# Masks of the first attention pass moved from TensorE to VectorE, second scores laid out by half of the rows, and loads and steps retimed

## What is computed

```
x = x + 0.5 * ffn(layernorm(x))
x = x + attn(layernorm(x))
x = x + 0.5 * ffn(layernorm(x))

ffn:  probs = softmax(x @ router_w.T)                 # 8 experts
      w = probs, kept up to a cumulated share of 0.9
      out = sum over e of (silu(x @ gate_w[e].T) * (x @ up_w[e].T)) @ down_w[e].T * w[:, e]   # 512 wide
attn: q, k, v with biases; 16 query heads, 4 key heads, 16 wide
      q, k: rms norm over the head, rotary embedding, q times a gain per head
      softmax of causal scores q k / 4, times v; output matrix and bias
```

## Time and profile before

| | |
|---|---|
| median of three runs | 1202.97 us (1202.05 to 1203.33) |
| the profiled execution | 1202.81 us, its span 1200.7 us |
| TensorE matmuls busy | 1161.9 us, 97% |
| VectorE, ScalarE, GpSimd busy | 817.4, 577.9, 667.5 us |
| mean granted TensorE clock | 0.996 |

### The profile page before, as it was taken

The page is one execution under the profiler, slowest core; times in us unless marked ns, Lnnn a source line. Parts: engine busy times, 40 slices in busy tenths (PEclk is TensorE's granted clock), DMA queues, the critical chain, the costliest instruction groups (busy, mean ns, idle before and its releaser), DMA issues.

```text
span 1200.7 us, 22926 instructions
## 1 busy us (share of the span) xinstructions
PE 1161.9 (97%) x8321; PEld 701.3 (58%) x8321; DVE 817.4 (68%) x1577; ACT 577.9 (48%) x954; POOL 667.5 (56%) x737
## 2 busy tenths in 40 slices
PE   4899999998999999999999999999999999999998
PEld 2455555665556566566566665566665656656655
DVE  6888896668777777577677577677667555554444
ACT  3544544444554554654554555555555454333332
POOL 3545443367477577576676666666655545332232
PEclk9899999999999999999999999999999999999999
DMA  4311210000000000000000000000000000000000
GB/s 176 127 53 53 68 52 1 1 1 2 1 1 2 1 2 1 1 1 2 1 1 1 1 1 2 5 15 1 1 2 1 19 1 2 1 14 5 1 1 19
DMA packets 10108, 19.26 MB, mean 16 GB/s; under 512 B 2192, under 2 KB 6800, under 8 KB 10000
## 3 DMA queue, kind: packets, MB, share of 16 engines
q1 hardware_dynamic: 9136, 15.17, 3.8%
q10 hardware_dynamic: 864, 2.63, 0.6%
HBM read 15.70 MB, written 2.10 MB: 15 GB/s over the span
## 4 chain that ended last, share of the span: by engine, by line
PE 71%; DVE 5%; POOL 4%; issue 2%; ACT 1%; DVEq 0%; ACTq 0%; POOLq 0%
PE YB L302 21%; PE G L283 20%; PE U L283 20%; POOL RR L1125 2%; PE S L438 2%; PE S L464 1%; PE S L479 1%; PE S L370 1%; PE S L414 1%; PE S L416 1%; DVE TS L705 1%; PE S L410 1%; DVE TS L710 1%; POOL HS L1069 1%; DVE MXN L944 1%
## 5 line engine op out<-in xcount | busy, mean ns | idle before, releaser
L1069 POOL TENSOR_TENSOR HS<-TS,HS 128x512 f16<-128x512 f32 x256 | 300.1, 1172 | 411.1 <-ACT HS L538 409.8
L302 PE MATMUL YB<-W,HS 128*128 128x256 f16 x3036 | 374.6, 273 | 13.8 <-DVE X L726 12.8
L283 PE MATMUL G<-XS,W 128*128 128x512 f16 x1536 | 376.7, 381 | 0.6 <-ACT XS L568 0.4
L283 PE MATMUL U<-XS,W 128*128 128x512 f16 x1536 | 375.2, 380 | 0.0
L302 PEld LDWEIGHTS YB<-W,HS 128*128 128x128 f16 x3036 | 293.0, 98 | 90.3 <-DVE X L726 18.3
L705 DVE SCALAR_TENSOR_TENSOR TS<-TS,G 128x512 f32<-128x512 f32 x256 | 175.2, 684 | 227.7 <-ACT TS L531 227.5
L538 ACT ACTIVATE HS<-TS 128x512 f16<-128x512 f32 x256 | 161.1, 629 | 265.0 <-DVE TS L710 262.9
L531 ACT ACTIVATE TS<-G,TSC 128x512 f32<-128x512 f32 x256 | 175.5, 686 | 209.1 <-PE G L283 199.3
L283 PEld LDWEIGHTS U<-XS,W 128*128 128x128 f16 x1536 | 150.7, 98 | 183.1 <-issue 2.8
L283 PEld LDWEIGHTS G<-XS,W 128*128 128x128 f16 x1536 | 147.2, 98 | 133.3 <-issue 3.4
L710 DVE SCALAR_TENSOR_TENSOR TS<-TS,U 128x512 f32<-128x512 f32 x256 | 175.9, 687 | 28.8 <-DVE TS L705 1.4
(11 more groups left out here) (181 smaller groups left out, 877.8 us busy)
## 6 DMA issues: line engine op xcount, KB each, us to landing
room<-in_up SPq DMA_DIRECT2D x4, 512.0 KB, 3.2
out_y<-X SPq DMA_DIRECT2D x16, 128.0 KB, 1.7
X<-in_x SPq DMA_DIRECT2D x3, 512.0 KB, 5.6
room<-in_gate SPq DMA_DIRECT2D x3, 512.0 KB, 3.2
room<-in_down SPq DMA_DIRECT2D x3, 512.0 KB, 3.6
QKT<-in_gate SPq DMA_DIRECT2D x3, 512.0 KB, 3.6
QKT<-in_up SPq DMA_DIRECT2D x3, 512.0 KB, 3.3
QKT<-in_down SPq DMA_DIRECT2D x3, 512.0 KB, 4.1
```

The source lines that it names most:

```text
L283: mm = eng.matmul(bank[:, :], W[:, e, wl, jj, kk * I + m * P:kk * I + (m + 1) * P], flat(XS16[:, b % 2, xl, kk, :, :], 'cq'), start=q == 0 ...
L302: mm = eng.matmul(out, HS[:, j % 2, hl, kk, m * P:(m + 1) * P], W[:, e, wl, 2, kk * D:(kk + 1) * D], start=kk + hl + wl == 0, stop=kk == K ...
L1069: eng.tensor_tensor(HS[:, j % 2, 1, m, :], TS[:, k % 3, :], HS[:, j % 2, 0, m, :], ALU.subtract).then_inc(L['g_lo'].sem, 1)
```

## The change

- **First scores.** `pe_max` has no mask matmuls and signals S0 and S1 separately. `dve_max` has one `tensor_tensor_reduce` for each head: scores plus mask, written back to the bank in place, with the negated extremum as a second output. `MB` gets a second, unmasked half for the 256 keys of an odd tile. `dve_mm` runs a slot later (`MM_STEP`).
- **Second scores.** S1 takes rows 64 to 127 and S0 rows 0 to 63 of key tile 0, both query tiles at once (512 columns, one matmul each). S2 still holds key tile 1 against query tile 1, with a matmul of each half of 256 columns, the second behind a wait. `pool_mask('a')` covers the query-tile-0 half of both blocks in one instruction, so `act_ph('b')` waits for it. `pe_pv` reads P in the new layout.
- **Steps.** The offsets of the conversions, of the rms norm (`sq`, `rb0`, `ss` a slot earlier), of `ax`, `ql`, `bo` and of the router change as the tables show; `dve_r2` is cut in two. `PREP` starts expert 2 at slot 8 and ends at 72 and 83.
- **Start.** SP issues all early loads: x 0 and 1, x 2 and 3, `gate`; after x 2 and 3 have landed, `up`, x 4 to 7, `down`, the router's weights, experts 1 and 2, then x's rest. ScalarE issues none. `pe_wb0(0)` stands ahead of the first transposes, and the third matrix's scale is found in slots 1 to 5, in YB.
- **Waits.** `s0_read`, `s1_read` and `s2_read` name only entries that used the bank. `RWR` and `LOW` are stored elsewhere or narrower.

```
-PREP = [-99, 0, 12, 24, 36, 47, 58, 69, 82]
+PREP = [-99, 0, 8, 24, 36, 47, 58, 72, 83]
...
+AT = {'at': (108, 114, 16, 33), 'qkv': (110, 116, 21, 39), 'qt': (117, 124, 30, 48), 'kt': (118, 125, 32, 48), 'q2': (125, 137, 48, 69)}
+MAX0 = (119, 122, 126, 128, 130, 132)
+MAXB = (38, 41, 50, 56, 59, 66)
+OUT = (5, 15)
+FTP0 = (3, 3, 6, 6)
+FIRST_FTP = (99, 102, 104, 109, 152, 152, 161, 161)
+FTP_LATER, ROUTE_LATER = (22, 24)
+ROUTE_FIRST = (3, 11, 112, 162)
+
+A_STEP = {'ax': 3, 'xl': 3, 'bo': 6}
+Q_STEP = {'rb1': 2, 'sq': 2, 'rb0': 2, 'rr': 3, 'r': 4, 'qn': 5, 'qz': 4, 'v': 5, 'qh': 6, 'ql': 6}
+I_STEP = {'eb': 1, 'ea': 1, 'ma': 2, 'ec': 2, 'hb': 3, 'mc': 3, 'ha': 4, 'lb': 4, 'hc': 5, 'la': 4, 'lc': 5, 'pv': 7, 'o': 8}
+R_STEP = {'r1': 1, 'ex': 1, 'r2': 1, 'r2b': 3, 'rank': 3, 'r3': 5}
+F_STEP = {'xn': 1, 'xh': 2, 'xl': 3}
+O_STEP = {'ot': 2, 'mm': 2, 'ad': 3}
+MM_STEP = 2
+
+W_FIRST = {'mx': 1, 'wt': 2, 'wr': 4, 'wb': 5, 'sc': 5, 'hi': 6, 'lo': 6}
...
-QKVP = by_tile(110, 116, 21, BATCH + 3)
-QTP = by_tile(118, 124, 30, BATCH + 12)
-KTP = by_tile(118, 124, 32, BATCH + 12)
-QTP2 = by_tile(125, 136, BATCH + 12, BATCH + 33)
...
-    MAXS += [[120, 122], [126, 128, 130, 132]][t_] if t_ < 2 else [[a_ + 3, a_ + 5], [a_ + 14, a_ + 21, a_ + 23, a_ + 30]][t_ % 2]
+    part = slice(2, 6) if t_ % 2 else slice(0, 2)
+    MAXS += MAX0[part] if t_ < 2 else [FIRST + BATCH * (t_ // 2 - 2) + s for s in MAXB[part]]
...
@@ pe_max, even tiles (odd ones alike)
-                        eng.matmul(bank[:, q * P:(q + 1) * P], QT1[rows(h), 2 * kv + q % 2, :], keys[rows(h), 0, kv, :], start=q == 0, stop=False, skip_group_check=True, tile_position=(64 * h, 0))
-                for bank in (S0, S1):
-                    mm = eng.matmul(bank[:, :].rearrange('p (g k) -> p g k', g=G), ident16[:, :], MB[:, :].unsqueeze(1).broadcast_to([P, G, P]), start=False, stop=True, skip_group_check=True)
+                        mm = eng.matmul(bank[:, q * P:(q + 1) * P], QT1[rows(h), 2 * kv + q % 2, :], keys[rows(h), 0, kv, :], start=q == 0, stop=q == 3, skip_group_check=True, tile_position=(64 * h, 0))
+                        if q == 3:
+                            mm.then_inc(L['p_mx'].sem, 1)
...
@@ pe_scores
-            part(S0, 0, 0, 0).then_inc(L['p_s0'].sem, 1)
-            part(S1, 0, 1, 1).then_inc(L['p_s0'].sem, 1)
-            part(S2, 1, 1, 1).then_inc(L['p_s0'].sem, 1)
-
-            eng.wait_ge(*L['p_s0'].at(i, 'b1'))
-            part(S1, 0, 1, 0).then_inc(lane.sem, 1)
-            eng.wait_ge(*L['p_s0'].at(i, 'a0'))
-            part(S0, 0, 0, 1).then_inc(lane.sem, 1)
-            eng.wait_ge(*L['p_s0'].at(i, 'c1'))
-            part(S2, 1, 1, 0).then_inc(lane.sem, 1)
+            part(S2, 1, (1,), 0).then_inc(L['p_s0'].sem, 1)
+            part(S1, 0, (0, 1), 1).then_inc(lane.sem, 1)
+            part(S0, 0, (0, 1), 0).then_inc(lane.sem, 1)
+
+            eng.wait_ge(*L['p_s0'].at(i, 'c0'))
+            part(S2, 1, (1,), 1).then_inc(lane.sem, 1)
...
@@ dve_max
-                if t % 2 == 0:
-                    x, out = (bank[:, :].rearrange('p (a g k) -> p a g k', a=2, g=2), MXN[:, 2 * j:2 * j + 2, :, h])
-                else:
-                    x, out = (bank[:, :].rearrange('p (g k) -> p g k', g=2), MXN[:, j, :, h])
-                eng.tensor_reduce(out, x, AX.X, ALU.max, negate=True).then_inc(L['v_mp'].sem, 1)
+                for g in range(heads):
+                    out = MXN[:, 2 * j + g // 2, g % 2, h:h + 1] if t % 2 == 0 else MXN[:, j, g, h:h + 1]
+                    x = bank[:, g * width:(g + 1) * width]
+                    mx = eng.tensor_tensor_reduce(x, x, mask, -1.0, 3.0e38, ALU.add, ALU.min, out)
+                mx.then_inc(L['v_mp'].sem, 1)
...
@@ SP's queue
+            x_load(0, 0, 2)
+            x_load(1, 2, 4)
+            sp_load(eng, 0, 0)
+
+            eng.wait_ge(s_x[1], 16)
+            sp_load(eng, 1, 0)
+            x_load(2, 4, 8)
+            sp_load(eng, 2, 0)
+            eng.dma_start(RW[:, :, :], d['rw']).then_inc(s_rw, 16)
+            for e in (1, 2):
+                for j in range(3):
+                    sp_load(eng, j, e)
...
@@ TensorE, ahead of slot 0
             pe_wt0(eng, 0)
-            for f in range(2):
-                pe_ftp(eng, f, FTP[0])
             pe_wb0(eng, 0)
-            for f in range(2, BT):
+            for f in range(BT - 1):
                 pe_ftp(eng, f, FTP[0])
             pe_wt0(eng, 1)
+            pe_ftp(eng, BT - 1, FTP[0])
             pe_wb0(eng, 1)
```

More of the change, by code:

```diff
@@ L56, with by_tile @@
 ITEM = [FIRST + PER * i for i in range(NI)]
-def by_tile(first, second, even, odd):
+def by_tile(name):
+    first, second, even, odd = AT[name]
     slots = [first, second]
@@ L244, in s0_read @@
             eng.wait_ge(*L['a_q2'].at(before(QTP2, s), 'q'))
-            eng.wait_ge(*L['a_fc'].at(before(FTP[:3 * BT], s), 'xs'))
-            eng.wait_ge(*L['v_pv'].at(before(ITEM, s, 7), 'rd'))
+            f = max((f for f in range(3 * BT) if (f % 2 == 0 or f >= 2 * BT) and FTP[f] < s), default=-1)
+            eng.wait_ge(*L['a_fc'].at(f, 'xs'))
+            pv_read(eng, s, (0, 1))
         def s1_read(eng, s):
@@ L263, in s2_read, with pv_read @@
             eng.wait_ge(*L['v_qb'].at(before(QKVP, s), 'qb'))
-            eng.wait_ge(*L['a_qc'].at(before(QTP, s), 'q'))
+            even = before(QTP[0::2], s)
+            eng.wait_ge(*L['a_qc'].at(2 * even if even >= 0 else -1, 'q'))
             eng.wait_ge(*L['a_kc'].at(before(KTP, s), 'k'))
             eng.wait_ge(*L['v_op'].at(before(OUTP, s), 'ad'))
-            eng.wait_ge(*L['a_fc'].at(before(FTP, s), 'xs'))
-            eng.wait_ge(*L['v_pv'].at(before(ITEM, s, 7), 'rd'))
-            eng.wait_ge(*L['v_ls'].at(before(ROUTE, s), 'ls'))
+            f = max((f for f in range(NT + NT) if (f % 2 == 1 if f < 2 * BT else f >= 3 * BT) and FTP[f] < s), default=-1)
+            eng.wait_ge(*L['a_fc'].at(f, 'xs'))
+            pv_read(eng, s, (3,))
+            if before(ROUTE, s) >= 3:
+                eng.wait_ge(*L['v_ls'].at(before(ROUTE, s), 'ls'))
+        def pv_read(eng, s, places):
+            i = max((i for i in range(NI) if i % 4 in places and ITEM[i] + I_STEP['pv'] < s), default=-1)
+            eng.wait_ge(*L['v_pv'].at(i, 'rd'))
         def pe_gu(eng, k):
@@ L496, in pe_slot @@
                 pe_scores(eng, i, s)
-            for i in due(ITEM, s, 7):
+            for i in due(ITEM, s, I_STEP['pv']):
                 pe_pv(eng, i, s)
@@ L512, in pe_slot @@
                 pe_op_tp(eng, t, s)
-            for t in due(OUTP, s, 2):
+            for t in due(OUTP, s, O_STEP['mm']):
                 pe_op_mm(eng, t)
@@ L651, in act_slot @@
         def act_slot(eng, s):
+            for f in due(FTP[:2 * BT], s, 1):
+                act_fc(eng, f)
             if s % 2 == 1:
@@ L684, in act_slot @@
                 act_ac(eng, t)
-            for t in due(QKVP, s, 6):
+            for t in due(QKVP, s, Q_STEP['qh']):
                 act_qh(eng, t)
@@ L998, in dve_slot @@
                 dve_max(eng, n)
+            for n in due(MAXS, s, MM_STEP):
                 if n in MAXN:
                     dve_mm(eng, MAXN.index(n))
-            for i in due(ITEM, s, 8):
+            for i in due(ITEM, s, I_STEP['o']):
                 dve_pv(eng, i)
@@ L1004, in dve_slot @@
                 dve_qb(eng, t)
-            for t in due(OUTP, s, 3):
+            for t in due(OUTP, s, O_STEP['ad']):
                 dve_op(eng, t)
@@ L1186, in pool_slot @@
                 pool_constants(eng)
-            for f in due(TILE, s, 3):
+            for f in due(TILE, s, F_STEP['xl']):
                 pool_f_xl(eng, f)
@@ L1316, in _ @@
             give_credit(eng, 'a_')
-            for e in range(2):
-                for j in range(3):
-                    if e or j != 1:
-                        eng.dma_start(RAW[e][:, j, :], d[('gate', 'up', 'down')[j]][e]).then_inc(s_w[e][j], 16)
-                if e == 0:
-                    eng.dma_start(RW[:, :, :], d['rw']).then_inc(s_rw, 16)
             for f in range(BT):
                 act_fx(eng, f)
-            for j in range(2):
-                act_fc(eng, 2 * j)
-                act_fc(eng, 2 * j + 1)
-                act_w(eng, 0, j)
+            act_fc(eng, 0)
+            act_w(eng, 0, 0)
+            for f in range(1, BT):
+                act_fc(eng, f)
+            act_w(eng, 0, 1)
             for s in range(SLOTS + 1):
@@ L1348, in _ @@
             dve_mx0(eng, 1)
-            for f in range(BT, BT + 2):
-                dve_f_stats(eng, f)
             dve_wr0(eng, 1)
@@ L1353, in _ @@
             dve_lo(eng, 0, 0)
-            for f in range(BT + 2, 2 * BT):
+            for f in range(BT, 2 * BT):
                 dve_f_stats(eng, f)
```

189 lines of the change are left out of this document (92 added, 97 removed), and 2 rows, old and new, of the table later.

## The result

The changed kernel takes **1164.54 us** (median of four runs, 1164.48 to 1165.05), the kernel before 1202.51 beside it (1201.9 to 1203.33): ratio 0.9685, 95% interval 0.9668 to 0.9702, 38.0 us less. The forecast was 1176, its range began at 1165: the direction was right, and the gain a little larger than the range allowed.

What follows compares the result with a forecast made beforehand. TensorE's queue was taken to bound the kernel: 1202.8 - 14.4 (masks) - 3.8 (second scores) - 6 (start) - 3 (first attention) - 1 (router steps) + 1.5 (stray stalls) = 1176 us, range 1165 to 1189 (its own 1167 to 1183).

Steps and rivals of the forecast that it cites:

- What bounds the kernel: Whole span: TensorE, busy 97% of 1200.7 us, is the limit; other engines count only where TensorE stands still.
- Part 1: First-score batches: the mask matmuls leave TensorE's queue, and all their 14.4 us should come off the span.
- Part 2: Second scores: four matmuls for six, less waiting, save 0.12 us an item, 3.8 us in all, between 0 and 8.3.
- Part 3: VectorE takes the masks: 37 us more work there, mostly covered by slack; retimed router steps -1 us, stray stalls +1.5.
- so +1.1 fits behind it: Even first-score batch: VectorE's added 1.1 us fits in the some 3.3 us of slack before TensorE needs YB.
- I count -1 us for all three: Router batch: later follow-ups gain 1.5; the batch's +0.6 and the moved ql and r2 count against; net -1 us.
- Part 4: The start: earlier gate weights and reordered first instructions bring the first low part to 13.8; 6 us saved, between 1 and 9.
- Part 5: First attention, 256 to 320 us: moved steps remove stalls such as a transpose waiting for GpSimd; 3 us, between 0 and 3.5.
- First rival: Score batches: a second instruction writes out the extremum, +2.3 us an even batch; VectorE takes back 11 us, 1187; chance 0.16.
- Second rival: Start and router: retiming gives nothing, waits only change places; the mask and second-score gains hold, 1185 us; chance 0.17.
- Slower: Long stretch: VectorE becomes the bound once new instructions average over 1.18 us; at 1.4 us the kernel takes 1242; chance 0.04.

Runs made afterwards that it cites:

- masks_only: The kernel before with only its masks moved to VectorE (and two small buffers to make room), all else as before: 1200.27 us, ratio 0.9979.
- more_vector: The changed kernel with an extra VectorE maximum over 384 constant elements ahead of each bank's masked maxima: 1171.47 us, ratio 0.9739.
- masks_only_quiet: The kernel before with masks on VectorE and GpSimd's subtraction for the hidden blocks' low part replaced by zero fill: 1187.18 us, ratio 0.9878.

## Why the prediction was wrong in size

- **What bounds the kernel**: right. Only what left TensorE's queue or its waits counted.
- **Part 1, masks, 14.4**: right to 0.1 us in the trace, and 13.3 when put back. But "all of it should come off the span" holds only with the new steps; alone in the old order 2.8 came off.
- **Part 2, scores, 3.8**: 4.6 to 4.8, inside its bounds.
- **Part 3, VectorE**: the price was too high (23.7 us for 37), the cover "so +1.1 fits behind it" right for a regular batch of the new order only (in the old one masks_only has seven more waits there, 4.8 us, beside the three of the router). The step that failed is "I count -1 us for all three and, for stray stalls from the added VectorE time elsewhere, +1.5". Measured in its place: the term is -9.2, and none of TensorE's 8.3 us of idle time in the long stretch is left. Put back alone, the follow-ups cost 3.9 there (forecast 1.5), the router's split 2.2 (forecast a cost), the spaced slots 3.2 and the norm's steps 1.2 (neither counted); these are prices in the new order and don't add up to the 9.2. The prediction had read the 8.3 us, put most of it down to the router batches, and still took off only 1 for them and added 1.5 of stalls elsewhere; no stray stall came. It also took for granted that what VectorE does beside GpSimd lasts as long in the new place. It does not: VectorE's busy time fell by 26 us for the same work. How much of the 9.2 comes from that and how much from the order itself stays open.
- **Part 4, start, 6**: 6.9. First G at 13.78 and first low part at 14.29 (13.8 forecast); the gate at 6.35 (6.0). The YB block was to come near 53 and came at 54.78. The loads gave 3 of it; the rest came less from the order (1 us) than from the router's split, 3.4 us, which the forecast had put only on the bad side. That the total came out near 6 is in part luck, and the granted clock at the start (some 10 us at half in one trace, 6.8 in the other) could move it by over 1 us, an estimate from half of the difference.
- **Part 5, 3**: 2.7.
- **First rival** (VectorE takes some back): its mechanism is true, two instructions each, and its price of +2.3 an even batch is not: +0.8, since they overlap. In the old order it would have been right: masks_only lost 11.5 us in the long stretch, near its 11, under a third of the load.
- **Second rival** (retiming gives nothing): it gave 1185; the steps are worth some 18 us even without the masks, the loads another 2.8.
- **Slower**: its point was 1.18 us an instruction, when VectorE's idle time is used up. more_vector shows that this is the wrong measure: TensorE lost time with VectorE at 72%.

## What to carry to other kernels

When work is given to an engine with slack, its idle share says nothing about whether it fits: read how late that engine is before the bounding engine's next need, batch by batch, and take the edit out of the new order and out of the old one separately. A retiming is priced by where each moved row lands beside the other engines' rows, too: look for one line and shape with two durations. And one wait a little longer than its neighbours can cost twice when the granted clock falls behind it.

## What the runs showed of the hardware

- A masked maximum of 128 elements is a row of 322 ns and an accumulator read of 138 ns, but the next masked maximum starts 0.25 us after the first; of 256 elements the row is 453 ns and the next starts 0.38 us after it.
- One comparison of 256 elements lasted 0.42 us alone and, six times of six in the kernel before, 1.38 us where GpSimd's subtraction was running when it began, ending 0.28 us behind it. Once, in the changed kernel, it lasted 0.41 beside the subtraction, and the subtraction 1.71 for 1.17.
- Behind single waits of 1.65, 2.06 and 2.11 us in the long stretch of masks_only the granted clock lay at half for 3.4 us; the twelve matmuls behind the last took 2.74 us for 1.49. Behind three waits of 1.87 and 1.88 us in the kernel before, one of 2.04 in masks_only and one of 2.59 in masks_only_quiet it stayed.
